# Softmax denominators later in the slot, inverse later still, router logits copied out of PSUM by VectorE, and the last block's first transposes moved ahead of its last output tiles

## The chip, the cores and the metric

One NeuronCore of one Trainium2 chip runs the whole kernel. The metric is the device time of that core in microseconds (us), median of three runs; the lower the better. Five engines run their own instruction streams in order: PE (TensorE, matmuls), DVE (VectorE), ACT (ScalarE), POOL (GpSimd) and SP (SyncE, which here only starts DMAs). They are coupled by semaphores alone, and the whole order of the work is written out by hand.

## The reference, cut to what matters

```python
B, S, D, H = 4, 1024, 512, 16          # attention: 16 heads of 32; experts: E=8, rank 64
xq, xk, xv = x @ wq.T, x @ wk.T, x @ wv.T
probs = softmax(einsum('bqhd,bkhd->bhqk', xq, xk), axis=-1)      # float32
x = layernorm(x + einsum('bhqk,bkhd->bqhd', probs, xv) @ wo.T)
logits = x @ Wr.T + br                                            # 8 per token
expert = argmax(softmax(logits)); weight = max(softmax(logits))
h = einsum('nd,erd->ner', x, A); y = einsum('ner,eor->neo', h, B) / 64
x = layernorm(x + y[expert] * weight)
```

All of it is float32. The softmax subtracts the row maximum, so the kernel computes the scores twice: once to find the maxima, once for the exponentials.

## The kernel before, in words

**Slots, units, halves.** The work is 32 slots; a slot s is one pair of heads of one batch (8 slots a batch), and is the grid on which everything else hangs. A slot has 16 units (8 blocks of 128 keys times 2 heads), and a unit has 2 halves (512 queries each), so a slot has 32 halves; "half 3 of slot 7" is a place in the order of every engine. In each half PE issues one score matmul into `sc[c]` (L815), one matmul for the maxima of a coming slot into one of three banks `mx` (L805), and one or two chunks of other work (projections L684, output projection L719, experts L735 to L763) into banks `w`. ACT takes the exponential of each score block into `P`, a ring of 7 units (L908). DVE reduces the `mx` banks (L1037). Every fourth unit, at halves 3, 11, 19 and 27, PE issues 8 matmuls of P with V into `pv` (L827).

**Denominators.** POOL adds up the exponentials of a slot, unit by unit, into a buffer `sums(s)` (L592 for the first of each chain, L595 after that): 14 adds in most slots, 12 in slots 0 to 3 and 31, where the last two units go to PE directly ("tail"). A unit of `P` can be overwritten only when its add is done. When POOL has added the last unit of slot s-1, `den(s-1)` on PE (L778: matmuls with ones) sums over the partitions, in half `den_at(s)` of slot s. Where two slots in a row use the same buffer, POOL's first add of the new slot (its place is half 5) waits for `den_done` of the old one. In slots 1 to 8 `den_at` is 3, except in slots 5 and 6, where it is 11.

**Their inverse.** After `den`: DVE copies the bank (`copy_den`, L1078), SP spreads four rows over 128 partitions one half later (`spread_den`, L492), DVE takes the reciprocal at +3 (L1089), SP stores it at +3 (`store_rec`, L497), SP waits for that store and loads it back, broadcast, at +4 (`load_rden`, L502), and POOL multiplies the attention output with it at +8 (`normalise`, L627, two instructions). SP is one in-order queue: while it waits in `load_rden`, nothing behind it is issued. Behind it are, among others, the stores of projected q and k (`store_qk`, L454). ACT splits the next q or k tile into the single buffer `split` only when the store of the tile before has landed (`hi_part`, L917). The loads of a later slot's q and k (`load_stack`, L460) stand at half 14; in slots 7 and 15 the load of 2 MB of x for the residual (`load_res`, L411) stands at half 16.

**Logits.** PE writes a tile's 8 logits into an `mx` bank (`lg`, L743); DVE adds the bias there, takes the maximum and marks the expert (`largest_logit`, L1156 to L1168, ending in `eq_done`); ACT takes the exponential from the bank with a sum (`softmax_sum`, L953, ending in `lexp_done`); DVE inverts the sum (L1174). The bank is free for PE at `lexp_done`. `softmax_sum` stands one or two halves after the matmul.

**The end.** After slot 31 the list `CLOSING` is worked off with seven banks in a ring, with a layer norm (POOL L604 to L609, ACT L958), a transpose `t1` and its copy (ACT L941), `lg`, `h`, `t2`, `z` for each of 8 tiles of 128 tokens.

Of the kernel before, what the change touches and what calls it, by code (L numbers as in the profile page):

```python
# [6 lines left out]
def build_attention_lora_moe_block(nc, xT, x, wqT, wkT, wvT, woT, aT, bT, wrT, br, out):  # L7
# [10 lines left out]
    E = br.shape[1]  # L18
# [4 lines left out]
    KB = S // 128  # L23
# [142 lines left out]
    def second(s):  # L166
        return s % 2 == 1 and (s < PAIRS - 1 or s > PAIRS * (B - 1))

    def tail(s):
        return s < 4 or s == LAST  # L170
# [7 lines left out]
    def den_at(s):  # L178


        return 11 if not tail(s - 1) and (second(s) != second(s - 1) or s % PAIRS == 2) else 3

# [32 lines left out]
    FIRST = KB * (B - 1)  # L215
    CLOSING = [("part", KB - 2), ("den", LAST), ("part", KB - 1)] + [("o", FIRST + t) for t in range(KB)]
    CLOSING += [("t1", FIRST), ("lg", FIRST), ("h", FIRST), ("t1", FIRST + 1), ("lg", FIRST + 1)]
    for t in range(KB):
# [11 lines left out]
    for batch in range(B):  # L230
        for kind in ("o", "z"):
            for t in range(0, KB, 2):
                alone = (batch, kind, t) == (B - 1, "z", KB - 2)
                for group in ([(t, 1), (t + 1, 1)] if alone else [(t, 2)]):
                    NORMS.append(group)
                    for m in range(group[1]):
                        NORM[kind, KB * batch + group[0] + m] = len(NORMS) - 1


    LOGITS = {}  # L240
    for half, done in ENDS.items():
        s, h = divmod(half + 1, HALVES)
        for kind, n in done:
            if kind == "lg":
                LOGITS.setdefault(half + (1 if s and h == den_at(s) else 2), []).append(n)

# [4 lines left out]
    with ctx:  # L251
# [12 lines left out]
        def sem(name):  # L264
# [26 lines left out]
        lmax, nlmax = sb("lmax", [128, 1]), sb("nlmax", [128, 1])  # L291
        lexp, lsum, lrec = sb("lexp", [128, E]), sb("lsum", [128, 2]), sb("lrec", [128, 4])
        eq, eqm = sb("eq", [128, E]), sb("eqm", [128, 1])
# [31 lines left out]
        FREED_BY = {"qk": lo_done, "v": v_done, "o": o_added, "part": part_added, "h": hm_done, "z": z_added, "t1": yT_done,  # L325
                    "t2": hmT_done, "lg": lexp_done, "xi": x_lo}
        BANK, BEFORE = {}, {}
# [47 lines left out]
        def norm_half(s):  # L375
            return HALVES * (s + 2) + 4 if s and s % PAIRS == 0 else den_half(s) + 8

# [12 lines left out]
        def _(sp):  # L390
# [130 lines left out]
            for half in range(HALVES * SLOTS):  # L521
# [31 lines left out]
                if h == 16 and p == 7 and b < B - 1:  # L553
                    load_res(b)
                for after, job in ((1, spread_den), (3, store_rec), (4, load_rden)):
                    if s and h == den_at(s) + after:
                        job(s - 1)
# [322 lines left out]
        def _(act):  # L880
# [67 lines left out]

            def softmax_sum(n, bank):
                act.wait_ge(eq_done, n + 1)  # L950
                if n > 1:
                    act.wait_ge(lrec_done, n - 1)
                act.activation(lexp[:, :], bank[:, E:2 * E], ACT.Exp, bias=nlmax[:, :], accum_out=lsum[:, n % 2:n % 2 + 1]).then_inc(lexp_done, 1)  # L953

# [32 lines left out]
            for half in range(HALVES * SLOTS):  # L987
                unit, c = divmod(half, 2)
                s, k = divmod(unit, UNITS)
                exp(unit, c)  # L990
                if half % HALVES == MAX_AT and s < LAST:
                    copy_max(s + 1)
                for n in LOGITS.get(half, ()):
                    softmax_sum(n, BANK["lg", n])
                if c == 1 and k == 1 and s:
                    copy_out(s - 1)
                for kind, n in ENDS.get(half, ()):
                    if kind == "qk":
                        hi_part(n)
                    elif kind == "v":  # L1000
                        copy_v(n)
                    elif kind == "t1":
                        copy_yT(n, BANK[kind, n])
                    elif kind == "t2":
                        copy_hmT(n, BANK[kind, n])
                if half in X_HIGH:
                    x_high(*X_HIGH[half])
                for kind, late in (("o", 7), ("z", 11)):
                    for m in range(2):
                        for n in ends(half - late + m, kind):  # L1010
                            if n % 2:
                                layer_norm(kind, n - m)
            copy_out(LAST)
            for kind, n in CLOSING:
# [6 lines left out]
                elif kind == "lg":  # L1021
                    softmax_sum(n, BANK["last", (kind, n)])
                elif kind == "t2":
                    copy_hmT(n, BANK["last", (kind, n)])
                    if t in (3, 5, 7):
                        for m in range(2):
                            layer_norm("z", FIRST + t - 3 + m)
# [4 lines left out]
        def _(dve):  # L1032
# [118 lines left out]
            def largest_logit(n, bank):  # L1151

                dve.wait_ge(lg_ready, n + 1)
                if n == 0:
# [3 lines left out]
                if n:  # L1158
                    dve.wait_ge(lexp_done, n)
                dve.tensor_reduce(nlmax[:, :], bank[:, E:2 * E], AX.X, ALU.max, negate=True).then_inc(lmax_done, 1)  # L1160
                dve.tensor_reduce(lmax[:, :], bank[:, E:2 * E], AX.X, ALU.max).then_inc(lmax_done, 1)
# [54 lines left out]
            for half in range(HALVES * SLOTS):  # L1216
# [21 lines left out]
                if s and h == den_at(s):  # L1238
                    copy_den(s - 1)
                for n in ends(half - 3, "lg"):  # L1240
                    inverse_sum(n)
                if s and h == den_at(s) + 3:
                    reciprocal(s - 1)
# [49 lines left out]
```

## Time and profile before

| | before |
|---|---|
| median of 3 runs | 1539.59 us (1538.74 to 1544.03) |
| the profiled execution | 1541.77 us, span 1540.0 us |
| PE busy | 96% of the span |
| POOL busy | 75% |
| DVE, ACT busy | 61%, 50% |

The span is from the first to the last record; the profiled execution's own time is 1.77 us longer. A row of the timeline gives start, duration, engine, line, output and input, the number of instructions merged, and in brackets how long the engine sat idle before it and what released it. A row of the windows gives the busy time of each engine in a stretch and PEclk, the granted clock of TensorE (1.00 is 2.4 GHz, 0.50 is 1.2 GHz).

### The profile page before, as it was taken

The page shows a single profiled execution, that of the slowest core. Times are in us where ns is not written, and L with a number is a line of the kernel's source. Part 1 is how long each engine was busy: PE and PEld are TensorE (multiplying, and loading weights), DVE is VectorE, ACT ScalarE, POOL GpSimd, SP SyncE. Part 2 cuts the span into 40 slices and gives each one's busy share as a digit, 9 for nine tenths or more (in the row PEclk, how much of TensorE's full clock was granted, in tenths as well). Part 3 has the DMA queues.
Part 4 walks back from the last instruction along what each step waited for, and adds up shares of the span by engine and source line. Part 5 has one row for each costly group of instructions (what it writes and reads, how often), then busy time and mean ns, then how long its engine had stood idle before and what let it go on. Part 6 is the DMA issues. An engine that isn't in the chain of part 4 may idle for free.

```text
span 1540.0 us, 20530 instructions
## 1 busy us (share of the span) xinstructions
PE 1480.7 (96%) x6872; PEld 865.1 (56%) x6872; DVE 932.6 (61%) x1722; ACT 776.8 (50%) x1421; POOL 1159.7 (75%) x654
## 2 busy tenths in 40 slices
PE   7999999989999999999999999999999999999998
PEld 5755456655645656556645555556664555554354
DVE  6756667655565566665566556666556666564633
ACT  3455555544555455545546445554555545455232
POOL 0376879978798867877889987777987888888301
PEclk9999999999999999999999999999999999899999
DMA  7355624444431422427242323324514222210001
GB/s 237 92 165 150 208 80 135 142 148 131 124 77 42 117 84 61 126 80 254 52 130 64 90 70 103 104 68 153 158 39 148 49 49 63 56 42 29 1 13 42
DMA packets 80217, 153.13 MB, mean 99 GB/s; under 512 B 19041, under 2 KB 26225, under 8 KB 79729
## 3 DMA queue, kind: packets, MB, share of 16 engines
q1 hardware_dynamic: 78720, 150.24, 33.5%
q8 instruction: 55, 0.90, 0.2%
q0 software_dynamic: 336, 1.07, 0.2%
q10 hardware_dynamic: 1056, 0.52, 0.1%
q14 instruction: 50, 0.40, 0.1%
HBM read 102.52 MB, written 48.49 MB: 98 GB/s over the span
## 4 chain that ended last, share of the span: by engine, by line
PE 78%; issue 7%; DVE 6%; POOL 4%; DMA 3%; ACT 1%; SPq 1%; POOLq 0%; ACTq 0%; DVEq 0%
PE w L684 14%; PE pv L827 13%; PE mx L805 13%; PE sc L815 13%; PE w L750 6%; PE w L763 6%; PE w L719 5%; DVE mxc L1037 3%; PE mx L778 2%; POOL Psum L595 2%; DMA spread_s<-den_s 1%; PE mx L743 1%; PE mx L763 1%; PE w L727 1%; DMA den_parts<-spread_s 1%
## 5 line engine op out<-in xcount | busy, mean ns | idle before, releaser
L1037 DVE TENSOR_REDUCE mxc<-mx 128x1 f32<-128x512 f32 x1024 | 683.8, 686 | 463.9 <-PE mx L805 460.8
L908 ACT ACTIVATE P<-sc 128x512 f32<-128x512 f32 x1024 | 598.8, 597 | 504.8 <-PE sc L815 490.6
L595 POOL TENSOR_TENSOR Psum<-Psum,P 128x1024 f32<-128x1024 f32 x296 | 695.7, 2383 | 26.5 <-ACT P L908 24.7
L815 PE MATMUL sc<-stack 98*128 98x512 f32 x1024 | 540.4, 530 | 7.5 <-ACT P L908 6.9
L805 PE MATMUL mx<-stack 96*128 96x512 f32 x1024 | 407.1, 402 | 9.1 <-DVE mxc L1037 4.6
L815 PEld LDWEIGHTS sc<-stack 98*128 98x128 f32 x1024 | 194.3, 190 | 142.7 <-issue 81.0
L805 PEld LDWEIGHTS mx<-stack 96*128 96x128 f32 x1024 | 195.9, 191 | 124.2 <-issue 70.8
L827 PE MATMUL pv<-P,V 128*32 128x512 f32 x2048 | 250.4, 607 | 0.0
L592 POOL TENSOR_TENSOR Psum<-P 128x1024 f32<-128x1024 f32 x50 | 118.6, 2390 | 132.7 <-ACT P L908 126.4
L684 PE MATMUL w<-xT_s,wqk_s 128*128 128x512 f32 x624 | 197.9, 408 | 12.0 <-DVE xT_s L1054 10.4
L684 PEld LDWEIGHTS w<-xT_s,wqk_s 128*128 128x128 f32 x624 | 116.9, 192 | 67.7 <-issue 43.4
L827 PEld LDWEIGHTS pv<-P,V 128*32 128x32 f32 x2048 | 57.9, 110 | 131.5 <-issue 108.9
L750 PE MATMUL w<-wide_f,turned_f 128*128 128x512 f32 x216 | 114.1, 617 | 0.0
L684 PE MATMUL w<-wide,xT_s 128*128 128x512 f32 x384 | 113.9, 400 | 0.0
L763 PE MATMUL w<-wide_f,turned_f 128*128 128x512 f32 x208 | 106.8, 599 | 0.1
L595 POOL TENSOR_TENSOR xT_s_f<-xT_s_f,P 128x1024 f32<-128x1024 f32 x41 | 98.1, 2415 | 9.9 <-ACT P L908 9.3
L719 PE MATMUL w<-wo_s,attT_f 128*128 128x512 f32 x196 | 101.3, 598 | 0.0
L627 POOL TENSOR_TENSOR attT_f<-pv_s,den_s 64x512 f32<-64x512 f32 x62 | 80.1, 1291 | 24.2 <-DMA den_s<-den_parts 14.6
L684 PEld LDWEIGHTS w<-wide,xT_s 128*128 128x128 f32 x384 | 71.2, 189 | 28.4 <-issue 13.3
L604 POOL TENSOR_TENSOR ve<-mv,eps_s 128x2 f32<-128x2 f32 (+1 forms) x33 | 6.5, 198 | 94.3 <-DVE mv L1126 94.3
L595 POOL TENSOR_TENSOR wo_s<-wo_s,P 128x1024 f32<-128x1024 f32 x32 | 75.3, 2397 | 1.2 <-ACT P L908 0.9
L929 ACT ACTIVATE pv_s<-pv 128x512 f32<-128x512 f32 x32 | 19.1, 598 | 82.2 <-PE pv L827 82.2
(147 smaller groups left out, 1086.8 us busy)
## 6 DMA issues: line engine op xcount, KB each, us to landing
stack<-qk_parts SPq DMA_DIRECT2D x186, 256.0 KB, 4.3
qk_parts<-split SPq DMA_DIRECT2D x56, 512.0 KB, 3.4
wqk_s<-wqk_parts SPq DMA_DIRECT2D x24, 512.0 KB, 4.5
xT_s_f<-xT SPq DMA_DIRECT2D x8, 1024.0 KB, 6.5
den_s<-den_parts SPq DMA_DIRECT2D x124, 64.0 KB, 2.1
r_f<-x SPq DMA_DIRECT2D x3, 2048.0 KB, 11.2
out<-r_f SPq DMA_DIRECT2D x12, 512.0 KB, 3.1
qk_parts<-turned SPq DMA_DIRECT2D x8, 512.0 KB, 3.9
```

The lines of the kernel that those rows point to most:

```text
L592: pool.tensor_tensor(sums(s)[:, i, :], P[:, (unit - 2) % NP, :], P[:, unit % NP, :], ALU.add).then_inc(add_done, 1)
L595: pool.tensor_tensor(sums(s)[:, i, :], sums(s)[:, i, :], P[:, unit % NP, :], ALU.add).then_inc(add_done, 1)
L627: pool.tensor_tensor(attT[64 * (p % 2):64 * (p % 2) + 64, p // 2, 512 * c:512 * c + 512], pv_s[64 * c:64 * c + 64, s % 2, :], den_s[64 * c ...
L684: return pe.matmul(bank[:, :], weights[i], moving[j], start=(c == 0), stop=(c == PASSES * KT - 1))
L719: done = pe.matmul(bank[:, :], attT[:, kt, 128 * t:128 * t + 128], wo_s[:, kt, :], start=(kt == 0 or only), stop=(kt == KT - 1))
L750: done = pe.matmul(bank[:, :], yT[:, 128 * kt:128 * kt + 128], a_s[:, kt, :], start=(kt == 0), stop=(kt == KT - 1))
L763: done = pe.matmul(bank[:, :], hmT[:, 128 * kt:128 * kt + 128], b_s[:, kt, :], start=(kt == 0), stop=(kt == KT - 1))
L805: pe.matmul(bank[:, :], stack(q, i)[0:3 * HD, 1, 128 * qb:128 * qb + 128], stack(q, i)[0:3 * HD, 0, 512 * c:512 * c + 512], start=True, st ...
L815: pe.matmul(sc[c][:, :], stack(s, i)[0:KS, 0, 128 * kb:128 * kb + 128], stack(s, i)[0:KS, 1, 512 * c:512 * c + 512], start=True, stop=True ...
L827: done = pe.matmul(pv[at:at + HD, :], V[:, kb, HD * head:HD * head + HD], P[:, (UNITS * s + 2 * kb + i) % NP, 512 * c:512 * c + 512], star ...
L908: act.activation(P[:, unit % NP, 512 * c:512 * c + 512], sc[c][:, :], ACT.Exp).then_inc(exp_done, 1)
L1037: dve.tensor_reduce(mxc[:, q % 2, at:at + 1], BANK["max", g][:, :], AX.X, ALU.max).then_inc(mx_done, 1)
```

## The change

Four things are changed.

1. `den` and `copy_den` go from half 3 to half 6 in slots 1 to 4, 7 and 8. The later slots keep 3 or 11.
2. The inverse stands later after `den` in every slot: reciprocal +7 instead of +3, store +8 instead of +3, load back +9 instead of +4, `normalise` +13 instead of +8 (but for the first slot of batches 1 to 3, whose `normalise` keeps its place, half 4 of the slot after next).
3. DVE copies the 8 logits to SBUF (one instruction more for each of 32 tiles); the bank is free at `eq_done`; ACT's `softmax_sum` reads the copy and stands four halves after the matmul (behind its old place), and the inverse of the sum six halves after.
4. In `CLOSING`, `t1`, `lg`, `h` of the first tile and `t1` of the second are laid among the last three output tiles.

```diff
     def den_at(s):
-        return 11 if not tail(s - 1) and (second(s) != second(s - 1) or s % PAIRS == 2) else 3
+        return 11 if not tail(s - 1) and (second(s) != second(s - 1) or s % PAIRS == 2) else 3 if s > PAIRS else 6
...
-    CLOSING = [("part", KB - 2), ("den", LAST), ("part", KB - 1)] + [("o", FIRST + t) for t in range(KB)]
-    CLOSING += [("t1", FIRST), ("lg", FIRST), ("h", FIRST), ("t1", FIRST + 1), ("lg", FIRST + 1)]
+    CLOSING = [("part", KB - 2), ("den", LAST), ("part", KB - 1)] + [("o", FIRST + t) for t in range(5)]
+    CLOSING += [("t1", FIRST), ("o", FIRST + 5), ("lg", FIRST), ("o", FIRST + 6), ("h", FIRST), ("t1", FIRST + 1), ("o", FIRST + 7)]
+    CLOSING += [("lg", FIRST + 1)]
...
-                    "t2": hmT_done, "lg": lexp_done, "xi": x_lo}
+                    "t2": hmT_done, "lg": eq_done, "xi": x_lo}
...
-            return HALVES * (s + 2) + 4 if s and s % PAIRS == 0 else den_half(s) + 8
+            return HALVES * (s + 2) + 4 if s and s % PAIRS == 0 else den_half(s) + 13
...
-                for after, job in ((1, spread_den), (3, store_rec), (4, load_rden)):
+                for after, job in ((1, spread_den), (8, store_rec), (9, load_rden)):
...
-                act.activation(lexp[:, :], bank[:, E:2 * E], ACT.Exp, bias=nlmax[:, :], accum_out=lsum[:, n % 2:n % 2 + 1]).then_inc(lexp_done, 1)
+                act.activation(lexp[:, :], logits[:, :], ACT.Exp, bias=nlmax[:, :], accum_out=lsum[:, n % 2:n % 2 + 1]).then_inc(lexp_done, 1)
...
-                for n in LOGITS.get(half, ()):
-                    softmax_sum(n, BANK["lg", n])
+                for n in ends(half - 4, "lg"):
+                    softmax_sum(n)
...
+                dve.tensor_copy(logits[:, :], bank[:, E:2 * E])
                 dve.tensor_reduce(nlmax[:, :], bank[:, E:2 * E], AX.X, ALU.max, negate=True).then_inc(lmax_done, 1)
...
-                for n in ends(half - 3, "lg"):
+                for n in ends(half - 6, "lg"):
                     inverse_sum(n)
-                if s and h == den_at(s) + 3:
+                if s and h == den_at(s) + 7:
                     reciprocal(s - 1)
```

The order of PE's instructions at the start of slot 7, before: `sc` are the scores, `mx<-stack` the maxima, `mx<-Psum,ones` the denominators of slot 6, `pv<-P,V` the last product of slot 6.

```order
L815 MATMUL sc<-stack 128x512
L805 MATMUL mx<-stack 128x512
L778 MATMUL mx<-Psum,ones 32x512 x4
L827 MATMUL pv<-P,V 32x512 x8
L684 MATMUL w<-xT_s,wqk_s 128x512 x2
L815 MATMUL sc<-stack 128x512
L805 MATMUL mx<-stack 128x512
```

And now, the same place (lines stand 7 lower in the changed file):

```order
L798 MATMUL mx<-stack 128x512
L820 MATMUL pv<-P,V 32x512 x8
L677 MATMUL w<-xT_s,wqk_s 128x512 x2
L808 MATMUL sc<-stack 128x512
L798 MATMUL mx<-stack 128x512
L677 MATMUL w<-xT_s,wqk_s 128x512
L808 MATMUL sc<-stack 128x512
L798 MATMUL mx<-stack 128x512
L677 MATMUL w<-xT_s,wqk_s 128x512 x2
L808 MATMUL sc<-stack 128x512
L798 MATMUL mx<-stack 128x512
L771 MATMUL mx<-Psum,ones 32x512 x4
```

The denominators moved behind the product and three more scores and maxima.

The order of SP's DMAs in slot 7, before, from the spreading of the denominators of slot 6 to the load of x and the next stores of q and k:

```order
L492 DMA spread_s<-den_s 32x1x16 x4
L497 DMA den_parts<-spread_s 128x16
L502 DMA den_s<-den_parts 32x512 x4
L454 DMA qk_parts<-split 128x2x512
L426 DMA wqk_s<-wqk_parts 128x1024
L460 DMA stack<-qk_parts 32x2x1024 x3
L411 DMA r_f<-x 128x8x512
L454 DMA qk_parts<-split 128x2x512 x2
```

And now:

```order
L485 DMA spread_s<-den_s 32x1x16 x4
L447 DMA qk_parts<-split 128x2x512
L419 DMA wqk_s<-wqk_parts 128x1024
L453 DMA stack<-qk_parts 32x2x1024 x3
L490 DMA den_parts<-spread_s 128x16
L495 DMA den_s<-den_parts 32x512 x4
L404 DMA r_f<-x 128x8x512
L447 DMA qk_parts<-split 128x2x512 x2
```

The store and the load back of the inverse moved from ahead of the weights' and the stacks' loads to behind them, and directly ahead of the load of x.

## Rows read from the trace of the kernel before

**Rows 1.** The page, part 1: busy time and share of the span.

```profile
PE 1480.7 (96%) x6872; PEld 865.1 (56%) x6872; DVE 932.6 (61%) x1722; ACT 776.8 (50%) x1421; POOL 1159.7 (75%) x654
```

**Rows 2.** Waits of PE: us in total, times, longest.

```profile
PE mx L778 <- POOL Psum L595: 8.0, 4, 7.0
PE sc L815 <- ACT P L908: 6.9, 6, 2.6
...
PE mx L805 <- ACT lexp L953: 2.2, 4, 0.9
...
PE mx L778 <- ACT lexp L953: 2.1, 2, 1.1
```

**Rows 3.** Timeline of PE, start of slot 7.

```profile
328.07 1.94 PE L778 MATMUL mx<-Psum,ones 128*32 128x512 f32 x8 [6.98 <-POOL Psum L595]
329.75 3.17 PE L827 MATMUL pv<-P,V 128*32 128x512 f32 x16
...
335.06 0.39 PE L815 MATMUL sc<-stack 98*128 98x512 f32 x1
```

**Rows 4.** Timeline of POOL, slots 5 to 7.

```profile
273.16 2.64 POOL L627 TENSOR_TENSOR attT_f<-pv_s,den_s 64x512 f32<-64x512 f32 x2 [1.16 <-issue]
...
311.60 16.32 POOL L595 TENSOR_TENSOR Psum<-Psum,P 128x1024 f32<-128x1024 f32 x7
335.23 4.76 POOL L592 TENSOR_TENSOR Psum<-P 128x1024 f32<-128x1024 f32 x2 [7.31 <-ACT P L908]
```

**Rows 5.** Windows of the scores (L815) alone: us, busy time of PE and PEld, PEclk, DMA.

```profile
259.61:293.90 34.29, 12.61 (x32) 6.04 (x32) 1.00 0.48 136
```

**Rows 6.** Windows: us; PE, PEld, DVE, ACT, POOL busy; PEclk, DMA share, GB/s.

```profile
1454.36:1456.93 2.57, 2.57 (x7) 1.09 (x6) 2.49 (x7) 1.52 (x2) 0.99 (x4) 1.00 0.00 0
1456.93:1473.61 16.68, 13.74 (x46) 8.01 (x45) 7.80 (x27) 5.09 (x11) 3.47 (x11) 0.80 0.01 1
328.00:333.00 5.00, 4.93 (x25) 1.28 (x26) 0.69 (x1) 0.01 (x1) 0.00 (x0) 0.57 0.01 1
359.60:363.20 3.60, 3.60 (x18) 0.64 (x17) 0.87 (x3) 0.54 (x1) 3.60 (x2) 0.53 0.81 264
```

**Rows 7.** Timeline of ACT and of PE, slot 7.

```profile
357.07 0.60 ACT L917 ACTIVATE split<-w 128x512 fp32r<-128x512 f32 x1 [3.17 <-DMA qk_parts<-split]
...
358.21 0.50 PE L815 MATMUL sc<-stack 98*128 98x512 f32 x1 [2.61 <-ACT P L908]
```

**Rows 8.** Timeline of SP's DMAs, slots 6 and 7.

```profile
300.70 0.34 SPq L497 DMA_DIRECT2D den_parts<-spread_s  x1
304.79 1.71 SPq L502 DMA_DIRECT2D den_s<-den_parts  x4
...
344.47 0.39 SPq L411 DMA_DIRECT2D r_f<-x  x1
347.22 0.38 SPq L454 DMA_DIRECT2D qk_parts<-split  x1
```

**Rows 9.** Waits of SP, DVE and POOL around the inverse.

```profile
SPq L502 <- DMA den_parts<-spread_s: 62.9, 31, 4.2
...
DVE spread_s L1089 <- DMA spread_s<-den_s: 7.0, 6, 2.5
...
POOL attT_f L627 <- DMA den_s<-den_parts: 14.6, 9, 2.6
```

**Rows 10.** Timeline of PE, slot 17.

```profile
800.87 0.50 PE L805 MATMUL mx<-stack 96*128 96x512 f32 x1 [1.29 <-DVE mxc L1037]
```

**Rows 11.** Timelines of POOL and of PE, slot 16.

```profile
752.79 4.77 POOL L592 TENSOR_TENSOR Psum<-P 128x1024 f32<-128x1024 f32 x2 [5.96 <-ACT P L908]
...
771.38 1.02 PE L719 MATMUL w<-wo_s,attT_f 128*128 128x512 f32 x2
```

**Rows 12.** Groups of instructions: busy us, mean ns, idle before.

```profile
L1156 DVE TENSOR_TENSOR mx<-mx,br_s 128x8 f32<-128x8 f32 x27 | 4.5, 165 | 3.0 <-PE mx L743 3.0
```

**Rows 13.** Timeline of ACT, closing part.

```profile
1455.23 1.52 ACT L958 ACTIVATE xT_s_f<-xT_s_f,nmr,rstd 128x512 f32<-128x512 f32 x2 [15.88 <-POOL nmr L609]
```

More of the change, by code:

```diff
@@ L237, in build_attention_lora_moe_block @@
                         NORM[kind, KB * batch + group[0] + m] = len(NORMS) - 1
[L240 to L245, printed above, removed]
     def ends(half, kind):
@@ L291, in build_attention_lora_moe_block @@
         lmax, nlmax = sb("lmax", [128, 1]), sb("nlmax", [128, 1])
-        lexp, lsum, lrec = sb("lexp", [128, E]), sb("lsum", [128, 2]), sb("lrec", [128, 4])
+        logits, lexp, lsum, lrec = sb("logits", [128, E]), sb("lexp", [128, E]), sb("lsum", [128, 2]), sb("lrec", [128, 4])
         eq, eqm = sb("eq", [128, E]), sb("eqm", [128, 1])
@@ L947, in copy_hmT, with softmax_sum @@
                 act.activation(hmT[:, :], bank[:, :], ACT.Copy, scale=SCALING).then_inc(hmT_done, 1)
-            def softmax_sum(n, bank):
+            def softmax_sum(n):
                 act.wait_ge(eq_done, n + 1)
@@ L1021, in _ @@
                 elif kind == "lg":
-                    softmax_sum(n, BANK["last", (kind, n)])
+                    softmax_sum(n)
                 elif kind == "t2":
```

## The prediction

> **What bounds the kernel now.** I read the page first: PE is busy 96% of the span, POOL 75% [rows 1]. Only a few per cent are to be had, where PE stands still or runs at its lower clock. Then the waits of PE [rows 2]: `den` waits for POOL's last add, 8.0 us in 4 times, and 7.0 of it is one event; scores wait for ACT's exponential, 6.9 us in 6; maxima and `den` wait for the logits' exponential, 4.3 us in 6. Then the timelines around the long ones. The 7 us are at the start of slot 7: `den` starts at 328.07 after 6.98 us idle, so PE had got there at 321.1 [rows 3]. The cause is that POOL is the slower engine in these slots. An add takes 2.33 us (7 in 16.32), `normalise` 2.64 [rows 4], so a slot of 14 adds is 35.3 us. The 32 scores of a slot take PE 34.3 us, 1.07 a half, at full clock [rows 5]. POOL falls behind by a microsecond a slot, and its last add of slot 6 ends at 327.92. PE is held meanwhile, no new scores are made, and so POOL then idles 7.31 us until the exponential of the new slot's third unit is there [rows 4]. Each makes the other wait. The stall also costs clock: from 328 to 333 the granted clock is 0.57, where it is 1.00 in the slots before [rows 5, 6].
>
> There is a second event in the same slot. At 358.21 PE has idled 2.61 us behind ACT, which stood 3.17 us until the store of a q or k tile had landed [rows 7], and the clock behind it is 0.53 [rows 6]. That store was issued at 347.22, behind the 2 MB load of x of 344.47 [rows 8].
>
> **The change, term by term**, against the profiled execution: span 1540.0 us, own time 1541.8.
>
> *Term 1, `den` at half 6.* From the start of the `pv` block to the end of the score of half 6 PE took 329.75 to 335.45, 5.7 us, of which about 1.3 is low clock (5 us at 0.57 lose 2.15, shared by `den` and the block) [rows 3, 6]. So without the stall PE is at the new place of `den` at 321.1 + 4.4 = 325.5. POOL's last add ended at 327.92. It now ends 1.16 us sooner, since the `normalise` at 273.16 that had to wait [rows 4] stands five halves later, and perhaps 0.5 sooner because scores of slot 4 no longer stand behind `den` (my estimate). `den` starts at 326.3 with 0.8 us idle instead of 7, and is done at 327.4, where the trace has PE at 335.45. Gain 8.0. If POOL ends no sooner and the shorter stall still brings low clock (3.4 us at half, 1.7), it is 4.7. I take 7.5. POOL starts the next slot at once, ends it at 327.4 + 35.3 = 362.7, and PE comes to `den` of slot 8 later than that (36 halves on, past 366): no new wait. In the other four slots `den` hardly waited for POOL; there the move is worth nothing, and what is moved is hidden by the same fillers.
>
> *Term 2, the store and the load back of the inverse, now at halves 14 and 15 in these slots.* In slot 7 they come directly behind the stack load and ahead of the load of x. SP waits in between for the store to land: from 300.70 to 304.79, 4.09 us, where a stack load stood ahead [rows 8], and on average 62.9/31 = 2.0 us, the others thus less [rows 9]. The four loads back then take 1.7 us to issue. So x is issued 5.8 us later relative to PE, and the store of the tile behind it too. The stack's bytes were still being moved when x was issued at 344.47, about 2 us of them (my estimate), so the tile's store lands some 4 us later, not 5.8. ACT's wait of 3.17 becomes 7, PE's of 2.61 about 6.6, and the low clock lasts some 0.3 us longer. Loss 4.3. At the least 1 (no delay behind the stack load), at the most 6.
>
> The Trainium skill, "DMA: Bandwidth & Descriptors", section "Queues, rings and completion order", says that a DMA's semaphore increment lands only after every earlier write of the same DMA engine. By that rule the small store is always as late as the stack load ahead of it, and the term is at its middle or above; without it it could be 1. The row of 4.09 us agrees with the rule.
>
> *Term 3, reciprocal and `normalise` later everywhere.* DVE waited 7.0 us in 6 times for the spread [rows 9]; PE felt that once, as 1.29 us [rows 10]. Four halves more (4.3 us) cover the longest, 2.5. Gain 1.3 (0.5 to 1.8). POOL's 14.6 us of waits for the load back [rows 9] go too, but PE waited for POOL at few of these places: nothing. What `normalise` must be ahead of is the next reader of `attT`. Tightest is slot 16: POOL starts its adds at 752.79, six of them end at 766.8, `normalise` at 769.5, and PE's first output tile is at 771.38 [rows 11]. 1.9 us are left. So nothing, but see rival C.
>
> *Term 4, the logits.* Of PE's 4.3 us behind the logits' exponential [rows 2], the bank now comes back a copy, not an exponential, after DVE's work. In most cases ACT goes right behind DVE and little is won, some 0.3 us; in the one of 0.9 us more. Together 1.8. The copy itself no row shows; nearest is the bias add of the same 128x8, 165 ns [rows 12]. 24 of them in the loop are 4 us of a DVE that is 61% busy; PE feels them only where it already waits for DVE, a few places: 0.7. Net gain 1.1. Bounds: a gain of 2.5 (all 1.8 and more, copies hidden), a loss of 2 (nothing won, every second copy felt).
>
> *Term 5, the closing order.* Before, three output tiles run from 1454.36 to 1456.93, and from there to the third transpose at 1473.61 it is 16.68 us, with PE busy 13.74 (2.94 idle) at a clock of 0.80, which is 3.3 us of lost clock: 10.4 us of work [rows 6]. Now the first transpose comes ahead of these three tiles and waits for its layer norm, which ACT starts at 1455.23 (two in 1.52 us) [rows 13]: PE idles from 1454.4 to 1456.1. Then 2.6 and 10.4 us of work, with the waits for the transposes' copies on ACT now beside output tiles and `h`. The third transpose is at 1469.1, 4.5 us sooner. If the idle 1.7 brings low clock, 2.8. I take 4.0. At most 5.
>
> Sum: 7.5 - 4.3 + 1.3 + 1.1 + 4.0 = 9.6. The profiled execution would be 1532.2. It was 2.2 us above the median of the runs, so the forecast is 1530.
>
> **The rivals.**
>
> *A: the load of x eats the gain.* Term 2 at 6, term 1 at 4.7, term 3 1.3, term 4 0, term 5 3: a gain of 3.0, 1536.5. For it: both sit in slot 7, on one SP queue, and each stall brings low clock. Against: the stack's load is soon through, and the delay is counted from it. It decides at a gap of over 5 us between the store and the load back of the inverse.
>
> *B: SP isn't held up.* Term 2 is 1, term 1 is 8, term 5 is 4.5: a gain of 15, 1525. Against it stands the row of 4.09 us, for it the mean of 2.0.
>
> *C: slower, through a late `normalise`.* In slots 16 and 24, and at the first partial tile of slot 31, a matmul reads what `normalise` writes. If it is 4.5 us later than I have it (POOL's adds paced by exponentials that come late), PE idles 2.6 us, and low clock adds up to 3.4, three times: 18 us against 9.6, 1548. From 1.9 us of lateness on there is a wait, and from 3 or so it outweighs the gain. Against it: POOL's rows are regular.
>
> *D: the cured stall comes back.* POOL is the slower engine from slot 4 to 8, so what PE wins at half 6 it gives back at the next wait for a free unit of `P`. Term 1 is 2: a gain of 4.1, 1535.5. Against it: POOL gets 7.3 us of idle time back at once, which is more than it lacks.
>
> **How the numbers follow.** Chances: the forecast 0.48 (own range 1526 to 1534), A 0.17, D 0.12, B 0.13, C 0.10. About 0.5%, 7.7 us, is what a measurement of this kernel can tell from no change: faster is below 1531.9, slower above 1547.3. The forecast is below the first in 0.7 of its cases, B always, A and D in one of ten: 0.34 + 0.13 + 0.03 = 0.50. Slower is half of C, 0.05. The rest, 0.45, is the same. The range goes from 1523 (B with term 5 at 5 and term 4 at 2) to 1539 (A with the copies felt) and leaves out most of C and the edges.
>
> **What the profile would show.** Term 1: the wait of `den` in slot 7 below 3 us, POOL's idle ahead of its first add there below 2. Term 2: over 4 us between the store and the load back of the inverse in slot 7, ACT's wait ahead of `split` above 5, PE's above 4. Term 3: no wait of DVE for the spread. Term 4: next to no wait of PE behind the logits' exponential, copies of 0.15 to 0.2 us. Term 5: 14.7 us from the end of the fifth output tile to the third transpose, where it was 19.25. I would be wrong if PE waits ahead of output tiles in slots 16, 24 or 31, if the tile's store in slot 4, now inside SP's wait, holds ACT as in slot 7, or if small stalls elsewhere bring other stretches of low clock.

## The result, and the profile after

The changed kernel took 1530.09 us (median of 4 runs, 1526.30 to 1530.94) beside 1540.74 of the kernel before (1538.74 to 1544.03): ratio 0.9924, 95% interval 0.9899 to 0.9949. Timed again later, 6 runs, it took 1530.95 beside 1540.80: ratio 0.9938 (0.9917 to 0.9960). The gain is 10.7 and 9.9 us by the medians, 11.7 and 9.5 us by the ratios; the forecast was a time of 1530.0 us, a gain of 9.6. The profiled execution is the 1526.3 one, with a span of 1524.5 us, so it lies 3.8 us below its median. A second profiled execution of the same kernel (*again*: span 1529.6) stands beside it where that matters.

Page, part 1, and the waits of PE, to be set beside [rows 1, 2] (lines are 7 lower in this kernel):

```profile
PE 1471.9 (97%) x6872; PEld 862.1 (57%) x6872; DVE 934.9 (61%) x1754; ACT 776.6 (51%) x1421; POOL 1158.7 (76%) x654
```

```profile
PE sc L808 <- ACT P L901: 11.1, 5, 7.1
...
PE mx L771 <- POOL Psum L588: 5.6, 6, 2.3
...
PE mx L771 <- DVE eq L1160: 0.7, 1, 0.7
PE mx L798 <- DVE eq L1160: 0.7, 1, 0.7
```

The waits behind `lexp` (4.3 us) are gone; 1.4 us behind `eq` stand in their place. That of `den` for POOL is down from one event of 7.0 to one of 2.3, but there are now six of them. That of the scores has grown from 6.9 to 11.1. Both large ones are in slot 7; timelines of PE and of ACT, beside [rows 3, 7]:

```profile
327.04 1.07 PE L771 MATMUL mx<-Psum,ones 128*32 128x512 f32 x8 [2.26 <-POOL Psum L588]
...
355.42 0.79 PE L808 MATMUL sc<-stack 98*128 98x512 f32 x1 [7.10 <-ACT P L901]
```

```profile
354.28 0.60 ACT L910 ACTIVATE split<-w 128x512 fp32r<-128x512 f32 x1 [7.67 <-DMA qk_parts<-split]
```

SP's DMAs in slot 7, beside [rows 8]: the inverse's store at 337.09 stands behind the stack load, and the load back can go out only 4.77 us later. Then comes x, then the tile's store, which lands 10.2 us after its issue (354.28 - 344.10):

```profile
335.78 1.26 SPq L453 DMA_DIRECT2D stack<-qk_parts  x3
337.09 0.43 SPq L490 DMA_DIRECT2D den_parts<-spread_s  x1
341.86 1.71 SPq L495 DMA_DIRECT2D den_s<-den_parts  x4
343.66 0.40 SPq L404 DMA_DIRECT2D r_f<-x  x1
344.10 0.58 SPq L447 DMA_DIRECT2D qk_parts<-split  x1
```

A load of x stands not only in slots 7 and 15 but in slot 23 too, and that of the last batch in slot 25. Only near the one in slot 7 does ACT wait over 1 us for the store of a tile.

Two windows of that stretch, beside [rows 6]. Behind the shortened wait of `den` the clock stays at 1.00 in this execution, where it was 0.57. In *again* it does not: there the `den` of slot 7 takes 1.94 us instead of 1.07, and the clock is at half for 3.4 us from 330.0 on. At the longer wait of the scores it is 0.50, that is 1.2 GHz, for 6.8 us, of which the first 2.6 lie still in the wait, where they cost nothing:

```profile
328.00:333.00 5.00, 5.00 (x29) 3.44 (x29) 4.38 (x7) 3.37 (x6) 4.72 (x3) 1.00 0.11 38
352.80:359.60 6.80, 4.18 (x14) 1.90 (x18) 2.86 (x5) 3.00 (x6) 5.82 (x3) 0.50 0.51 166
```

POOL's first add of slot 7 waits 1.38 us instead of 7.31 [rows 4]. In slot 8 it waits 7.04, now for `den` itself:

```profile
328.28 4.75 POOL L585 TENSOR_TENSOR Psum<-P 128x1024 f32<-128x1024 f32 x2 [1.38 <-PE mx L771]
...
374.85 4.75 POOL L585 TENSOR_TENSOR Psum<-P 128x1024 f32<-128x1024 f32 x2 [7.04 <-PE mx L771]
```

The closing part, timeline of PE. The fifth output tile ends at 1443.94; the first transpose has idled 1.33 us; the third transpose starts at 1458.11:

```profile
1442.06 1.88 PE L712 MATMUL w<-wo_s,attT_f 128*128 128x512 f32 x4
1445.27 0.63 PE L728 MATMUL mx<-ident,xT_s_f 128*128 128x128 f32 x4 [1.33 <-ACT xT_s_f L951]
...
1458.11 0.60 PE L728 MATMUL sc<-ident,xT_s_f 128*128 128x128 f32 x4
```

### The profile page after: what moved, and what is told of

Read it like the earlier page. It is cut to its first block, busy times and chain, and to the rows that moved or that the text cites. A ratio compares the mean times of both kernels' runs of the same rounds, so it can differ in the third digit from the quotient of the medians.

```text
span 1524.5 us, 20562 instructions
## 1 busy us (share of the span) xinstructions
PE 1471.9 (97%) x6872; PEld 862.1 (57%) x6872; DVE 934.9 (61%) x1754; ACT 776.6 (51%) x1421; POOL 1158.7 (76%) x654
## 3 DMA queue, kind: packets, MB, share of 16 engines
q0 software_dynamic: 336, 1.07, 0.2%
## 4 chain that ended last, share of the span: by engine, by line
PE 78%; issue 8%; POOL 6%; DVE 4%; DMA 2%; ACT 1%; SPq 0%; POOLq 0%; ACTq 0%; DVEq 0%
PE w L677 14%; PE pv L820 13%; PE sc L808 13%; PE mx L798 13%; PE w L712 6%; PE w L756 5%; PE w L743 5%; POOL Psum L588 3%; PE mx L771 2%; DVE mxc L1030 2%; POOL attT_f L620 1%; POOL Psum L585 1%; PE mx L756 1%; PE w L720 1%; PE mx L736 1%
## 5 line engine op out<-in xcount | busy, mean ns | idle before, releaser
L808 PE MATMUL sc<-stack 98*128 98x512 f32 x1024 | 539.4, 529 | 11.6 <-ACT P L901 11.1
L743 PE MATMUL w<-wide_f,turned_f 128*128 128x512 f32 x208 | 108.4, 607 | 0.0
L756 PE MATMUL w<-wide_f,turned_f 128*128 128x512 f32 x208 | 106.9, 599 | 0.1
```

Of the source, the lines that this page charges most:

```text
L743: done = pe.matmul(bank[:, :], yT[:, 128 * kt:128 * kt + 128], a_s[:, kt, :], start=(kt == 0), stop=(kt == KT - 1))
L756: done = pe.matmul(bank[:, :], hmT[:, 128 * kt:128 * kt + 128], b_s[:, kt, :], start=(kt == 0), stop=(kt == KT - 1))
L808: pe.matmul(sc[c][:, :], stack(s, i)[0:KS, 0, 128 * kb:128 * kb + 128], stack(s, i)[0:KS, 1, 512 * c:512 * c + 512], start=True, stop=True ...
```

## The experiments

Twelve kernels ran. The first four are the kernel before with one part of the change each.

**1. `den` alone.**

```
-        return 11 if ... else 3
+        return 11 if ... else 3 if s > PAIRS else 6
```

> The kernel before with the first part alone: denominators and their copy at half 6 in slots 1 to 4, 7 and 8, the inverse at its old distances (+3, +3, +4, +8). Theory: the 7 us wait in slot 7 shrinks to about 2.5 us, and since the store and load back of the inverse now stand at halves 9 and 10, ahead of the stack load, the load of x is not delayed: ACT's wait for the tile's store stays near 3.2 us. Gain 5 to 7 us, ratio 0.996. Rival (the x load suffers from any later den): ACT's wait is 7 us here too and the gain is 1 to 3 us.

Measured: 1537.38, ratio 0.9985 (0.9971 to 0.9999), a gain of 2.3. Timelines of PE and ACT of this kernel:

```profile
330.74 1.06 PE L778 MATMUL mx<-Psum,ones 128*32 128x512 f32 x8 [2.52 <-POOL Psum L595]
...
356.87 0.80 PE L815 MATMUL sc<-stack 98*128 98x512 f32 x1 [4.94 <-ACT P L908]
```

```profile
355.73 0.60 ACT L917 ACTIVATE split<-w 128x512 fp32r<-128x512 f32 x1 [5.50 <-DMA qk_parts<-split]
```

The wait of `den` is shortened, as expected, and the wait behind the tile's store has nearly doubled (2.61 before), though the distances of the inverse are as they were. My theory of 5 to 7 us failed by this; the rival had the gain right (1 to 3).

The starts of two executions can't be compared as they stand: this one lost 3.4 us of clock near 90 us and the one before none. So times are taken from the end of column A of the table below (191.66 before, 193.63 here). Counted so, PE comes to the wait 5.6 us sooner (at 158.3, before 163.9), but x goes out only 1.9 us sooner (150.9, 152.8), and the tile's store lands 3.3 us sooner (162.1, 165.4); the rest, 2.3 us, is the longer wait. What holds SP is again the time between the inverse's store and its load back. The store now goes out right behind a tile's store (335.09) and a load of weights (335.78) of 512 KB each, and the load back can go 3.83 us later, where it was 1.46 before:

```profile
336.47 0.59 SPq L497 DMA_DIRECT2D den_parts<-spread_s  x1
340.30 1.73 SPq L502 DMA_DIRECT2D den_s<-den_parts  x4
```

**2. The inverse alone.**

```
-            return HALVES * (s + 2) + 4 if s and s % PAIRS == 0 else den_half(s) + 8
+            return HALVES * (s + 2) + 4 if s and s % PAIRS == 0 else den_half(s) + 13
...
-                for after, job in ((1, spread_den), (3, store_rec), (4, load_rden)):
+                for after, job in ((1, spread_den), (8, store_rec), (9, load_rden)):
...
-                if s and h == den_at(s) + 3:
+                if s and h == den_at(s) + 7:
```

> The kernel before with the second part alone: reciprocal +7, store +8, load back +9, normalise +13, denominators at their old places. Theory: DVE's wait for the spread goes (1.3 us of PE), but POOL's multiply now stands after idle time that it used to fill, so the next slot's denominators wait some tenths of a us for POOL in several slots; together between a gain of 1.5 and a loss of 1.5 us, ratio 0.999 to 1.001. The 7 us wait in slot 7 shrinks by about 1 us. Rival: the later inverse is what cures the kernel, gain over 4 us.

Measured: 1540.14, ratio 1.0003 (0.9988 to 1.0019). DVE no longer waits for the spread, the 1.29 us of [rows 10] are gone, and `den` of slot 7 waits 6.34 us instead of 6.98. But the slot-7 wait behind the tile's store grows here too, with a gap of 3.69 us between the inverse's store and load back:

```profile
359.71 0.79 PE L815 MATMUL sc<-stack 98*128 98x512 f32 x1 [4.95 <-ACT P L908]
```

**3. The logits alone.**

```
-                    "t2": hmT_done, "lg": lexp_done, "xi": x_lo}
+                    "t2": hmT_done, "lg": eq_done, "xi": x_lo}
...
+                dve.tensor_copy(logits[:, :], bank[:, E:2 * E])
```

> The kernel before with the third part alone: logits copied by VectorE, bank free at eq_done, exponential four halves after. Theory: PE's 4.3 us of waits behind the logits' exponential fall to about 1.5 us behind eq, the copies of 0.15 us are hidden: gain 1 to 3 us, ratio 0.999. Rival: the 24 copies are felt and it is 1 to 2 us slower.

Measured: 1536.92, ratio 0.9977 (0.9964 to 0.9990), a gain of 3.5, a little above the 1 to 3 expected. PE's waits behind `lexp` are gone. But POOL takes some of it back: the kernel before has 0.94 us behind `lexp` at 485.63 and no wait of `den` in the next slot, this one the reverse, and the same in a later slot. At 887.00 the `den` that had waited 1.02 us for `lexp` (885.90 before) now waits 1.10 for POOL:

```profile
514.77 1.07 PE L771 MATMUL mx<-Psum,ones 128*32 128x512 f32 x8 [0.81 <-POOL Psum L588]
...
610.75 1.07 PE L771 MATMUL mx<-Psum,ones 128*32 128x512 f32 x8 [0.60 <-POOL Psum L588]
...
887.00 1.06 PE L771 MATMUL mx<-Psum,ones 128*32 128x512 f32 x8 [1.10 <-POOL Psum L588]
```

**4. The closing order alone.**

```
-    CLOSING = ... + [("o", FIRST + t) for t in range(KB)]
+    CLOSING = ... + [("o", FIRST + t) for t in range(5)]
+    CLOSING += [("t1", FIRST), ("o", FIRST + 5), ("lg", FIRST), ("o", FIRST + 6), ...]
```

> The kernel before with the fourth part alone: the closing order. Theory: the end is 4 to 5 us shorter (one idle time of 1.3 us instead of 0.8 and 2.2, and no low clock in front of the third transpose), ratio 0.997. Rival: a stretch of low clock follows the new idle time, gain 2.5 to 3 us. If the parts were independent, the four gains would add up to the 11.7 us of the whole; by the theory they add up to more (by about 4 us), because only the whole delays the load of x.

Measured: 1535.53, ratio 0.9982 (0.9968 to 0.9995), a gain of 2.8 by time. In the profiled execution the closing part is 5.8 us shorter (column D below), of which 5.1 are low clock that doesn't come. Its first transpose waits longer than in the changed kernel, without a cost that shows:

```profile
1454.15 0.63 PE L736 MATMUL mx<-ident,xT_s_f 128*128 128x128 f32 x4 [2.17 <-ACT xT_s_f L959]
```

The four gains (2.3, -0.5, 3.5, 2.8) make 8.1, the whole 9.5 to 11.7 by its two ratios. They add up within the intervals; that the parts are worth more together can neither be shown nor excluded.

The next four are the changed kernel with one thing altered.

**5. x loaded later.** The load goes to slot 8, half 4, ahead of its first reader by some 50 us.

```
-                if h == 16 and p == 7 and b < B - 1:
+                if h == 4 and s == PAIRS:
+                    load_res(0)
+                if h == 16 and p == 7 and 0 < b < B - 1:
                     load_res(b)
```

> This is the changed kernel with the first batch's 2 MB load of x issued in slot 8 at half 4 instead of slot 7 at half 16; its first reader is some 50 us later. Theory (the load of x holds back the tile's store behind it, and that is term 2): ACT's wait of 7.67 us ahead of split and PE's of 7.10 us in slot 7 are gone (below 1), no low clock there. Without the stall POOL, which idles 3.8 us in the slot, ends it at about 364.0 and PE comes to den of slot 8 at about 363 to 364, so up to 1 us is given back there. Gain against the changed kernel 7 to 9 us: about 1522, ratio to before 0.987 to 0.988. Rival (the store waits for something else, the stack load or the inverse's store): the wait of PE stays above 4, ratio 0.991 to 0.993. Rival (POOL or a later stall gives it back): the wait in slot 7 is gone, den or scores wait for POOL 4 us or more in slots 8 to 10, ratio 0.990.

Measured: 1520.27, ratio 0.9866 (0.9842 to 0.9891), which is 9 or 11 us better than the changed kernel by its two ratios (7 to 9 expected). The wait of 7.10 us is gone: ACT's `split` follows its work with no idle time, and PE has no wait of over 0.5 us between `den` of slot 7 and that of slot 9, where 0.62 us went back to POOL:

```profile
353.62 0.60 ACT L912 ACTIVATE split<-w 128x512 fp32r<-128x512 f32 x1
```

```profile
331.14 1.94 PE L773 MATMUL mx<-Psum,ones 128*32 128x512 f32 x8 [2.37 <-POOL Psum L590]
...
410.85 1.06 PE L773 MATMUL mx<-Psum,ones 128*32 128x512 f32 x8 [0.62 <-POOL Psum L590]
```

**6. The inverse's store one half sooner**, ahead of the stack load.

```
-                for after, job in ((1, spread_den), (8, store_rec), (9, load_rden)):
+                for after, job in ((1, spread_den), (7, store_rec), (9, load_rden)):
```

> The changed kernel with the store of the inverse one half sooner (7 instead of 8 halves after den), so that it goes out ahead of the stack load and not behind it. Theory (the store behind the stack load is what holds SP 4.8 us): the time from the store's issue to the load back stays 4 or more in slot 7 because the stack load now stands between them, but the store has landed sooner, so x goes out 1.5 to 3 us sooner relative to PE and ACT's wait before split falls from 7.7 to 5 or 6; gain 1 to 3 us, ratio 0.991. Rival (the store of this small tile is slow by itself): nothing moves, wait 7 to 8, ratio 0.992 to 0.993.

Measured: 1523.94, ratio 0.9887 (0.9865 to 0.9909). SP in slot 7:

```profile
338.90 0.34 SPq L490 DMA_DIRECT2D den_parts<-spread_s  x1
339.40 1.26 SPq L453 DMA_DIRECT2D stack<-qk_parts  x3
340.70 1.81 SPq L495 DMA_DIRECT2D den_s<-den_parts  x4
```

Three stack loads are issued in between, and still the load back goes out 1.80 us after the store, not 4.77: I was wrong that the gap would stay at 4. Yet with 3 us of the gap gone, ACT's wait before `split` falls only from 7.67 to 6.41 (5 to 6 expected) and PE's to 5.85. From the issue of x to the landing of the tile's store it is 12.4 us here, 10.6 in the changed kernel: x now goes out close behind the stack loads. The gain of 6 to 8 us, by the two ratios of the changed kernel, is above the 1 to 3 that I had expected. Beside *again* the table below shows 4.0 of it in B and 3.0 in C, where this execution has two stretches of low clock less. Less lost clock the gain is 2.5; whether the edit spares the low clock or chance did, these runs don't show.

**7. The inverse back where it was, 8. `den` back at half 3**, each in the changed kernel (the lines of 2 and 1, reversed).

> The changed kernel with the reciprocal, the store and load back and normalise where they were before (3, 3, 4 and 8 halves after den), all other parts kept. Theory (the later inverse costs 2 to 4 us in slot 7 through the load of x and wins 1 to 2 by the spread's waits elsewhere): PE's wait in slot 7 is about 5 as with den alone (4.94) instead of 7.1; 1 us of waits for the spread comes back near the place of 800; ratio 0.991 to 0.993. Rival (the parts help each other: once den and the logits are moved, the spread and the load back are late at several places and hold PE): 3 us or more slower than the changed kernel, ratio 0.9945.

> The changed kernel with den back at half 3 in slots 1 to 4, 7 and 8, all other parts kept. Theory (den at half 6 was worth about 2 us alone, since 5 of its 7.5 came back as the wait for the tile's store): PE waits 6 to 7 us for den in slot 7 and 3.5 to 5 in front of the score behind the store; ratio 0.9935 to 0.995. Rival (with the inverse moved too, den's place is worth its whole 7.5): ratio 0.997.

Measured: 1529.28, ratio 0.9923 (0.9898 to 0.9948), and 1530.66, ratio 0.9936 (0.9912 to 0.9959). Neither can be told from the changed kernel (0.9924, 0.9938). PE's waits behind the tile's store in slot 7:

```profile
355.38 0.80 PE L808 MATMUL sc<-stack 98*128 98x512 f32 x1 [5.42 <-ACT P L901]
```

```profile
360.13 0.80 PE L808 MATMUL sc<-stack 98*128 98x512 f32 x1 [5.33 <-ACT P L901]
```

So the first of the two moves adds about 2.5 us to that wait and the second 1.9: 2.1, 2.6 and 3.4 with neither (the closing order alone, before, the logits alone), 4.9 to 5.4 with one, 7.0 and 7.1 with both. The gap between the inverse's store and its load back goes the same way: 1.46 or 1.47 with neither, 3.67 to 3.83 with one, 4.77 and 4.63 with both.

**9. The changed kernel again.**

> The changed kernel itself, so that it stands beside the kernels built on it. If the parts add up (2.3 for den, 0 for the inverse, 3.5 for the logits, 2.8 for the closing order, each timed alone, 9 us together), ratio 0.994; if the parts are worth more together than alone, 0.992 or below.

Its numbers stand at the top.

**10. Both repairs, 5 and 6, together.**

> The changed kernel with both repairs, the load of x in slot 8 and the store of the inverse ahead of the stack load. Theory: with the load of x out of the way the store of the tile isn't late in either order, so the earlier store of the inverse adds at most 1 us to the later load of x: ratio 0.986 to 0.987, no wait of PE above 1 us behind the exponential in slot 7. Rival (the early store had a gain of its own, in all 31 slots): 2 us or more below the later load of x alone, ratio 0.985 or less.

Measured: 1519.59, ratio 0.9865 (0.9840 to 0.9890): as with x alone, so what the early store brings beside x is not to be told from nothing. POOL takes some back in slot 11, where the wait was 0.84:

```profile
499.64 1.06 PE L773 MATMUL mx<-Psum,ones 128*32 128x512 f32 x8 [2.41 <-POOL Psum L590]
```

**11. `den` of slot 7 at half 8, 12. and that of slot 8 back at half 3.**

```
-        return ... else 3 if s > PAIRS else 6
+        return ... else 3 if s > PAIRS else 8 if s == PAIRS - 1 else 6    # 11
+        return ... else 3 if s >= PAIRS else 8 if s == PAIRS - 1 else 6   # 12
```

> As the run before, with den of slot 7 at half 8 instead of 6. Theory: POOL's last add ends 2.4 us after PE has come to half 6 there, and two halves are 2.15 us of work: den waits below 0.6, and the low clock of 3.4 lost half-speed us (1.7 us) behind it is gone; gain 2 to 4 us, ratio 0.984 to 0.9855. Rival (POOL is the slower engine, so it gives all of it back at den of slot 8 or 9): den of slot 8 or 9 waits 2 us more, gain below 1, ratio 0.986 to 0.987.

> As the run before, with den of slot 8 back at half 3. Theory: in slot 8 POOL stands 1.4 us before its first add until den has been made, though its own last add was over; with den at half 3 it starts sooner, and the waits for POOL behind it (0.6 us in slot 9) go: gain 0 to 1.5 us. Rival (POOL's last add isn't over at half 3 once the stall of slot 7 is gone): den of slot 8 waits 2 to 3 us with low clock behind it, 3 us slower than the run before.

Measured for 11: 1516.84, ratio 0.9849 (0.9824 to 0.9874), the fastest of all. The wait of `den` in slot 7 is gone, but slot 8 has one of 1.43 where 10 has none over 0.5, and by the table the stretch is no shorter than in 10 (280.25, 280.35). Its lead of 2.7 us in the medians lies within the intervals. So POOL takes the gain back, as the rival said. For 12: 1527.27, ratio 0.9911 (0.9891 to 0.9932), 10 us slower than 11 (6.8 in B, of which 3.4 are low clock). Here my theory, a gain of up to 1.5 us, was wrong; the rival came, at three times its size. The stall of [rows 3] is back nearly whole, one slot later, POOL's idle time behind it too:

```profile
366.92 1.94 PE L773 MATMUL mx<-Psum,ones 128*32 128x512 f32 x8 [6.61 <-POOL Psum L590]
```

```profile
374.66 4.77 POOL L587 TENSOR_TENSOR Psum<-P 128x1024 f32<-128x1024 f32 x2 [7.88 <-ACT P L903]
```

**All profiled executions side by side**, in us, worked out from PE's timelines: A, from the start to the maximum that waits 0.7 for `xT_s` (191.66 before); B, from there to the score of slot 10 that waits 2.3 for ACT (484.19); C, to the first output tile of the closing part, which waits 2.2 (1448.27); D, to the last tile of `z` that waits 0.8 (1529.95). "Lost" is the time lost to low clock: the sum, up to the end of D, over windows of 8.5 us, of 8.5 times (1 - granted clock), good to 0.3 us. It counts low clock while PE stands idle too, up to 2.8 us of it. "Rest" is the span less that.

```
                       A       B       C      D     span   lost    rest
before               191.7   292.5   964.1   81.7  1540.0  20.5  1519.5
1  den               193.6   290.8   961.2   78.3  1534.0  15.1  1518.9
2  inverse           191.2   294.8   958.6   81.6  1536.2  20.3  1515.9
3  logits            191.8   295.7   953.6   81.7  1532.9  13.5  1519.4
4  closing           193.5   293.2   960.7   75.9  1533.4  13.5  1519.9
changed              190.8   290.6   956.3   76.8  1524.5  11.9  1512.6
9  changed again     194.1   291.9   956.4   77.0  1529.6  17.0  1512.6
5  x late            194.6   285.1   957.9   75.9  1523.5  15.3  1508.2
6  store early       193.6   287.9   953.4   77.0  1522.0  11.9  1510.1
7  old inverse       191.7   291.5   959.0   76.0  1528.2  15.3  1512.9
8  den at 3          191.2   295.1   955.3   77.1  1528.8  17.0  1511.8
10 5 and 6           192.1   280.4   958.2   77.1  1517.8  10.2  1507.6
11 den of 7 at 8     194.3   280.3   959.9   75.9  1520.4  11.8  1508.6
12 den of 8 at 3     194.3   287.1   958.0   77.0  1526.4  15.3  1511.1
```

The low clock can be taken out of each column in the same way, and this says more than the last two columns. From the start to 479 us the kernel before and experiments 3 and 4 are the same program, and still B less its lost clock is 287.4, 288.9 and 289.8 in them: a single execution can't tell less than some 2.4 us there. C is steadier. Less lost clock it is 953.8, 953.9 and 954.3 without the later inverse and the new logits, 951.9 with either alone (950.5 with the logits in experiment 7), and 949.4 to 950.0 with both in four executions of five (948.7 in experiment 8; the three with `den` waiting 2.4 us in slot 11 have 951.2 to 951.4). D is 76.5 to 76.7 with the old closing order and 74.3 to 75.9 with the new one.

## Why the prediction was right

The sum was a gain of 9.6; measured are 11.7 and 9.5 by the ratios. The total held; how it is made up held only in part.

**Terms 1 and 2** (7.5 and -4.3, net 3.2). Column B answers for both: with neither it is 292.5, 293.2 and 295.7 (mean 293.8), with both 290.6 and 291.9 (mean 291.3): 2.5 us. By the place of `den` alone, with x where it was, it is 294.3 at half 3 (five kernels) and 291.2 at half 6 (four): 3.1 us, of which 2.7 are low clock; timed alone, `den` gained 2.3. The mechanism is as written: the stall of `den` fell from 7 to between 2.1 and 2.6 us (1.47 in experiment 6; forecast 0.8, but PE was there at 324.8, 0.7 us sooner than reckoned, and POOL's last add ended at 326.9, 1.0 us sooner than before and not 1.7), POOL got its idle time back, and ACT's wait for the tile's store grew to 7.67 and PE's to 7.10 (forecast 7 and 6.6), with a gap of 4.77 us between store and load back (forecast 4.1). In the trace of before that gap is long where a stack load stands right ahead of the store, as at 300.70, and short in slot 7:

```profile
298.73 1.41 SPq L460 DMA_DIRECT2D stack<-qk_parts  x3
...
336.60 0.35 SPq L497 DMA_DIRECT2D den_parts<-spread_s  x1
338.06 1.73 SPq L502 DMA_DIRECT2D den_s<-den_parts  x4
```

Experiment 6 bears this out: with the store ahead of the stack load it is 1.80. Experiment 1 widens it: a tile's store and a load of weights ahead do nearly the same (3.83), and so x was late there too, though the inverse's store stands ahead of the stack load. The Trainium skill, "DMA: Bandwidth & Descriptors", section "Queues, rings and completion order", has a semaphore increment land only after every earlier write of the same DMA engine; the 4.77 and the 1.80 us agree with it. They would agree as well with a small store whose own bytes wait behind the larger ones, and no run here tells the two apart.

The sum of term 2 can be redone, counted from the end of A: x went out at 152.8 in both kernels while PE came to its wait 6.5 us sooner (157.5, before 163.9), where the forecast had x 5.8 us later relative to PE. The tile's store then landed 10.6 us after x's issue, not 12.6; these are the 2 us of the stack's bytes. 6.5 less 2.0 is 4.5, and by that the wait grew.

What was wrong in term 2 is whose loss it is. I put all of it down to the inverse's halves. Experiments 1, 2, 7 and 8 show about 2.2 us for each of the two moves. With `den` at half 6 alone PE arrives 5.6 us sooner, while SP, whose chain of spread, store and load back hangs on `den`, sends x only 1.9 us sooner. The gain of term 1 is for the most part spent there: less lost clock B is 287.7 on average with `den` at half 3 and 287.4 at half 6. This is why `den` moved by itself or moved back is worth so little.

That x is what the tile's store stands behind was an assumption of the prediction; experiment 5 shows it. Without x in its way the wait is gone, and B is 5.5 and 6.8 us shorter. By time the gain is 11 us by the later ratio of the changed kernel (0.9938) and 9 by the first (0.9924); less lost clock the table has 4.4. Rival A had the right mechanism (x eats the gain), not the right size.

**Term 3** (1.3). The waits for the spread are gone. By time the edit is worth nothing (1.0003 alone, 0.9923 without it), because the loss in slot 7 belongs to it too. In C, which leaves slot 7 out, it gains 2.0 us alone and 1.0 beside the others (949.4 and 949.6, 950.5 in experiment 7), all less lost clock: the term itself was about right. Rival C didn't come: no wait of over 0.5 us ahead of an output tile in slot 16, 24 or 31, other than the 2.18 that was there before.

**Term 4** (1.1, at most 2.5) was mis-sized. The copy takes 167 ns, as estimated from the 165 of [rows 12]; timed alone the part gains 3.5 (1.4 to 5.5). The waits won were more than the 1.8 us of the forecast, since of 4.3 us only 1.4 came back behind `eq`, but POOL took 2.5 at `den` (0.81, 0.60 and 1.10). PE's idle time over C is 17.5 before, 16.3 with the logits alone and 14.9 in the changed kernel. By the last two columns, the single execution of experiment 3 has all its gain in low clock (13.5 lost, 20.5 before) and none in the rest (1519.4, 1519.5), but by column it is otherwise: C less its lost clock is 1.9 us shorter (951.9, 953.8), and the 1.5 us that B is longer can hardly be the logits', whose first matmul is at 482, 5 us ahead of B's end. So about 2 us of the 3.5 are shown in the place where the edit acts. Whether short waits that go away spare stretches of low clock too, or that execution had fewer by chance, these runs don't settle.

**Term 5** (4.0, between 2.8 and 5). From the end of the fifth output tile to the third transpose it is 14.2 us (1443.94 to 1458.11) where it was 19.25; 14.7 was forecast. D is 75.9 to 77.1 in all ten executions with the new order, and 81.6 to 81.7 in three of the four with the old; in the fourth it is 78.3, since only one stretch of low clock fell there. Less lost clock D is 1.5 and 1.3 us shorter in the two executions of the changed kernel; the other 3.4 are low clock that doesn't come. Timed alone: 2.8 (0.8 to 4.9).

**Rival D** (the cured stall comes back) is true in small and, as experiment 12 shows, in large. POOL is the slower engine, and each microsecond that PE wins ahead of `den` is paid in part at a later one: 0.84 in slot 11 of the changed kernel, which comes from the logits (0.81 in experiment 3, none over 0.5 in experiment 1), and 2.41 in experiment 10. It didn't come back in slot 8 because there, too, `den` now stands at half 6. In the changed kernel that looks useless, since POOL waits 7.04 us for it; once x is out of the way it is worth the 10 us between 11 and 12. I had written "no new wait" for slot 8 and not seen that this hung on the place of `den` there. The reason that I gave is miscounted besides: from half 6 of slot 7 to half 6 of slot 8 it is 32 halves, not 36. That it comes out near is luck: where nothing stalls, in experiment 10, the two `den` are 37.5 us apart, POOL's last add ends at 364.9, and `den` starts at 365.07.

**Rival B** is added up wrongly: 8 - 1 + 1.3 + 1.1 + 4.5 is 13.9, not 15, and its time 1525.7. The lower end of the range, which starts from it, should have been 1524; the result lies far from both.

Of the whole gain the table gives 6.9 us in the rest (1519.5, 1512.6 twice) and 3.5 to 8.6 in low clock, depending on the execution. The near match of 1530.09 with 1530.0 is luck in part, as the places show. Terms 3 and 4 put 2.4 us into C, and in both executions of the changed kernel C is 7.7 or 7.8 us shorter, of which 4.2 to 4.4 stand less lost clock. The other 3.4 are low clock that experiments 1 and 4, which change nothing there, lose too: the execution of the kernel before had two stretches more by chance. In A, where I had put the move of `den` at nothing, PE stands idle some 1.5 us less with `den` at half 6 (6.2 to 6.4 us behind its first matmul in nine executions, 7.6 to 8.1 with half 3 in five).

## What to carry to other kernels

When a stall is cured, look at what the released engine will meet next at its new, earlier time: here a tile's store behind a 2 MB load whose issue did not move. A large load that nobody reads for 50 us belongs where no store that is waited for stands behind it; moving that one line was worth 9 or 11 us, about as much as the four edits of this change together (9.5 or 11.7). A wait of an engine for a late instruction can be idle time that costs nothing today, and the reserve that the next repair needs: try it again after each.

## What the runs showed of the hardware

The same kernel, profiled twice (changed, and again), had spans of 1524.5 and 1529.6 us. The 5.1 us between them are all in the granted clock: less the lost time both are 1512.6. The losses sit at the same few points of the program in most executions, nearly all of 1.7 or 3.4 us each (5.1 at the stall of `den` in experiments 2 and 8), at the half clock of 1.2 GHz, and whether a point has one differs: 3.4 us near 90 us in the second execution and none in the first. A single profile of this kernel can't tell changes of under some 5 us by its span. Its span less the lost time is better, but not free of chance: B of three executions whose program is the same up to 479 us differs by 2.4 us even so (287.4 to 289.8), C of three by 0.5 (953.8 to 954.3).

The time from the store of a small tile to the load that waits for it is 1.80 us with the store ahead of the three stack loads of 256 KB each, and 4.77 or 4.63 (the second execution of the changed kernel) behind them, on one queue. Behind a store and a load of 512 KB each, issued within 1.4 us ahead of it, it is 3.67 to 3.83 (four kernels), and 1.46 in slot 7 of the kernel before.
